# Linear attention and experts on one core: scores of two quads in five visits instead of six, the next batch's x turned earlier

## What is computed

```python
qf, kf = taylor_exp(q), taylor_exp(k)          # 16 heads, 16 features a head
A = tril(qf @ kf.T)                            # 512 x 512 for each batch and head
y = (A @ v) / (sum over past of qf . kf + EPS)
attention = y @ Wo.T
logits = xn @ Wg                               # 8 experts, the best two for each token
ffn = sum over top 2 of gate * (silu(xn @ W1[e].T) * (xn @ W2[e].T)) @ W3[e]
out = x + attention + ffn
```

## Time and profile before

| what | value |
|---|---|
| median of three runs | 640.49 us (639.61 to 642.61) |
| profiled execution | 641.93 us |
| its span, first to last instruction | 640.1 us |
| granted TensorE clock, mean | 0.998 |
| busy, share of the span | PE 96%, PEld 74%, DVE 70%, ACT 54%, POOL 56% |
| a batch of the attention stage (quad 0 of batch 3 to quad 0 of batch 4) | 35.15 us |

### The profile page before, as it was taken

The page is one execution under the profiler, slowest core; times in us unless marked ns, Lnnn a source line. Parts: engine busy times, 40 slices in busy tenths (PEclk is TensorE's granted clock), DMA queues, the critical chain, the costliest instruction groups (busy, mean ns, idle before and its releaser), DMA issues.

```text
span 640.1 us, 16670 instructions
## 1 busy us (share of the span) xinstructions
PE 615.1 (96%) x5181; PEld 475.5 (74%) x5181; DVE 450.3 (70%) x1134; ACT 348.0 (54%) x515; POOL 360.3 (56%) x453
## 2 busy tenths in 40 slices
PE   8899999999999999998899899999999999999995
PEld 8565665666666666655788788888888888888884
DVE  6876878787787776587787466666666667666663
ACT  3678878787878777775564233333333333333331
POOL 4265564737364654657167366566666666656645
PEclk9999999999999999999999999999999999999999
DMA  4753554545544444552953465656655656656553
GB/s 133 176 121 102 132 159 112 152 95 153 137 103 124 99 121 100 159 140 89 334 149 65 100 126 119 121 119 126 126 117 125 120 120 126 120 120 122 123 96 43
DMA packets 73347, 80.37 MB, mean 126 GB/s; under 512 B 12368, under 2 KB 61392, under 8 KB 73264
## 3 DMA queue, kind: packets, MB, share of 16 engines
q1 hardware_dynamic: 56144, 50.72, 30.1%
q0 software_dynamic: 16704, 28.12, 22.2%
q10 hardware_dynamic: 416, 0.46, 0.3%
HBM read 27.72 MB, written 22.95 MB: 79 GB/s over the span
## 4 chain that ended last, share of the span: by engine, by line
PE 43%; issue 26%; POOL 17%; DVE 8%; POOLq 2%; ACT 2%; DMA 0%; DVEq 0%; ACTq 0%
PE banks L1171 10%; POOL xg L544 9%; PE banks L1153 8%; PE banks L1191 7%; POOL out L570 6%; PE banks L1297 5%; PE banks L1200 4%; PE banks L1235 4%; POOL mark L556 3%; POOLq L554 2%; PE banks L1318 2%; PE banks L1220 2%; PE banks L1226 1%; ACT T L607 1%; DVE xTl L828 1%
## 5 line engine op out<-in xcount | busy, mean ns | idle before, releaser
L570 POOL DMA_INDIRECT out<-yo,xw x71 | 112.6, 1586 | 103.8 <-DVE yo L1100 99.9
L535 POOL TENSOR_SCALAR_AFFINE_SELECT T<-T 128x512 f32<-128x512 f32 x128 | 81.2, 646 | 108.6 <-ACT T L613 45.0
L1297 PE MATMUL banks<-w12h,xgh 128*128 x284 | 113.0, 398 | 3.4 <-DVE xgl L1078 3.3
L1297 PE MATMUL banks<-w12l,xgh 128*128 x284 | 111.4, 392 | 0.0
L1297 PE MATMUL banks<-w12h,xgl 128*128 x284 | 111.0, 391 | 0.0
L1112 DVE TENSOR_TENSOR hs<-banks,hs 128x512 f32<-128x512 f32 x71 | 49.1, 692 | 85.2 <-PE banks L1297 81.0
L706 ACT ACTIVATE sTh<-banks 128x512 fp32r<-128x512 f32 x71 | 42.4, 599 | 93.4 <-DVE banks L1088 76.8
L544 POOL DMA_INDIRECT xg<-xs_scr,glist x71 | 71.8, 1012 | 24.5 <-issue 19.7
L1171 PE MATMUL banks<-T,vau 128*17 128x512 f32 (+3 forms) x1024 | 75.5, 434 | 0.3 <-POOL T L535 0.3
L526 POOL DMA_INDIRECT xs_scr<-xb,slots x64 | 63.6, 994 | 19.0 <-issue 12.5
L1153 PE MATMUL banks<-Q,K 32*128 32x256 f32 (+2 forms) x1024 | 70.0, 358 | 2.0 <-DMA K<-Kt 1.8
(11 more groups left out here) (186 smaller groups left out, 1245.6 us busy)
## 6 DMA issues: line engine op xcount, KB each, us to landing
hq<-hs SPq DMA_DIRECT2D x244, 64.0 KB
w12r<-w SPq DMA_DIRECT2D x16, 512.0 KB, 4.4
Q<-Q SPq DMA_DIRECT2D x126, 64.0 KB, 2.4
out<-xa SPq DMA_DIRECT2D x16, 256.0 KB
w3r<-w SPq DMA_DIRECT2D x8, 512.0 KB, 7.1
K<-Kt SPq DMA_DIRECT2D x126, 32.0 KB
xa<-x SPq DMA_DIRECT2D x7, 512.0 KB, 4.8
xg<-xs_scr,glist POOLq DMA_INDIRECT x71
```

The source lines that it names most:

```text
L535: e.affine_select(out=v, in_=v, pattern=[[0, 4], [1, P]], compare_op=ALU.is_ge, fill=-1.0, base=0, channel_multiplier=-1).then_inc(s["g_mk ...
L570: e.indirect_dma_start(out, bass.IndirectOffsetOnAxis(xw[:, t % XR, NE:NE + 1].bitcast(U32), 0), yo[:, t % 2, :], None, compute_op=ALU.add ...
L1297: i = e.matmul(banks[:, 2 * (t % 2) + m, :], a[:, k, :], w[:, bass.ds(expert[t] * 4 + (2 * k + m), 1), :], start=(k == 0 and n == 0), stop ...
```

## The change

The last key block (3) moves from part 2 to part 1, where it fills the free 128 columns of the banks, now with matmuls of 128 columns. Part 2 then holds key block 2 alone, 256 columns, and is done for both quads of a pair at once, in the even quad: two quads have five visits. T1 and T2 have 4 x 512 columns each, the squares follow (`group` numbers the visits), and the masks of both quads in T2 are made in the even quad. The third visit of an even quad waits for the moves of both halves. The x steps of batches 2 to 7 go from `slot_b` to `slot_a` of quad 1, ahead of the second visit on all engines. yw moves to free space elsewhere, since T1 and T2 grew. In an odd quad the second send stands between the two T1 masks.

```diff
 def slot_a(n):
-    return [("C", 0, 0), ("f", 1, 6)] if n == 0 else []
+    b, qd = divmod(n, 4)
+    if n == 0:
+        return [("C", 0, 0), ("f", 1, 6)]
+    return [("x", b + 1, 0), ("x", b + 1, 1)] if qd == 1 and 0 < b < LAST else []
...
-        steps = [("x", b + 1, 0), ("x", b + 1, 1)] if b else [("v", 1, 0)]
+        steps = [] if b else [("v", 1, 0)]
...
+def group(n, part):
+    return 5 * (n // 2) + 3 * (n % 2) + part
...
-        T1 = r1.take("T1", 1536, F32, (4, 384))
-        T2 = r2.take("T2", 1536, F32, (4, 384))
-        yw = [r1.take("yw0", 512), r2.take("yw1", 512)]
+        T1 = r1.take("T1", 2048, F32, (4, 512))
+        T2 = r2.take("T2", 2048, F32, (4, 512))
+        ry = Region(Q1, Q1 + 1024)
+        yw = [ry.take(f"yw{u}", 512) for u in range(2)]
...
+            def masks(n):
+                b, qd = divmod(n, 4)
+                mask(n, T0[n % 2][:, :, 0:P], 0)
+                if sends_after(n, 0):
+                    send(*sends_after(n, 0))
+                mask(n, T1[:, :, 0:P], 1)
+                if sends_after(n, 1):
+                    send(*sends_after(n, 1))
+                mask(n, T1[:, :, 384:512], 1)
+                if qd == 2 and b < NBATCH - 2:
+                    root(b + 2)
+                if n % 2 == 0:
+                    mask(n, T2[:, :, 0:P], 2)
+                    mask(n, T2[:, :, 256:384], 2)
+                if sends_after(n, 3):
+                    send(*sends_after(n, 3))
...
             def squares1(n):
...
-                    e.activation(T1[:, 2 * h:2 * h + 2, :], banks[:, 2 * h:2 * h + 2, 0:384], ACT.Square, scale=0.25,
+                    e.activation(T1[:, 2 * h:2 * h + 2, :], banks[:, 2 * h:2 * h + 2, :], ACT.Square, scale=0.25,
...
-                squares2(n)
+                if n % 2 == 0:
+                    squares2(n)
...
-                jobs = (((0, 0, 512),), ((1, 0, 384),), ((3, 0, 256), (2, 256, 256)))[part]
-                for j, (jm, c0, w) in enumerate(jobs):
+                jobs = (((h, 0, 0, 512),), ((h, 1, 0, 384), (h, 3, 384, 128)), ((0, 2, 0, 256), (1, 2, 256, 256)))[part]
+                if part == 2:
+                    e.wait_ge(s[f"d_q{g}1"], MOVES * (b + 1))
+                    e.wait_ge(s[f"d_k{g}1"], MOVES * (b + 1))
+                for j, (hj, jm, c0, w) in enumerate(jobs):
...
-                scores(n, 2)
+                if n % 2 == 0:
+                    scores(n, 2)
```

More of the change, by code:

```diff
@@ L527, in send, with mask @@
                                          xb[b % 2][:, blk, :], None).then_inc(s[f"d_xs{b % 2}"], 16)
-            def mask(n):
-                b, qd = divmod(n, 4)
[L531 to L538, removed]
+            def mask(n, v, part):
+                e.wait_ge(s["a_s"], 2 * group(n, part) + 2)
+                e.affine_select(out=v, in_=v, pattern=[[0, 4], [1, P]], compare_op=ALU.is_ge, fill=-1.0, base=0,
+                                channel_multiplier=-1).then_inc(s["g_mk"], 1)
+            def masks(n):
+                b, qd = divmod(n, 4)
+                mask(n, T0[n % 2][:, :, 0:P], 0)
[12 more added lines that the diff above has]
+                    send(*sends_after(n, 3))
             def gather(t):
@@ L574, in gpsimd_program @@
             for n in range(NQ):
-                mask(n)
+                masks(n)
             done(e, "G", 0, 0)
-            e.wait_ge(s["p_s"], 6 * NQ)
+            e.wait_ge(s["p_s"], 5 * NQ)
             e.wait_ge(s["d_xs0"], 512)
@@ L595, in squares0 @@
                 for h in range(2):
-                    e.wait_ge(s["p_s"], 6 * n + h + 1)
+                    e.wait_ge(s["p_s"], 2 * group(n, 0) + h + 1)
                     if n >= 2 and h == 0:
@@ L603, in squares1 @@
                 for h in range(2):
-                    e.wait_ge(s["p_s"], 6 * n + h + 3)
+                    e.wait_ge(s["p_s"], 2 * group(n, 1) + h + 1)
                     if n and h == 0:
                         e.wait_ge(s["p_av"], n)
-                    e.activation(T1[:, 2 * h:2 * h + 2, :], banks[:, 2 * h:2 * h + 2, 0:384], ACT.Square, scale=0.25,
+                    e.activation(T1[:, 2 * h:2 * h + 2, :], banks[:, 2 * h:2 * h + 2, :], ACT.Square, scale=0.25,
                                  bias=1.0).then_inc(s["a_s"], 1)
@@ L611, in squares2 @@
                 for h in range(2):
-                    e.wait_ge(s["p_s"], 6 * n + h + 5)
-                    e.activation(T2[:, 2 * h:2 * h + 2, :], banks[:, 2 * h:2 * h + 2, P:512], ACT.Square, scale=0.25,
+                    e.wait_ge(s["p_s"], 2 * group(n, 2) + h + 1)
+                    e.activation(T2[:, 2 * h:2 * h + 2, :], banks[:, 2 * h:2 * h + 2, :], ACT.Square, scale=0.25,
                                  bias=1.0).then_inc(s["a_s"], 1)
@@ L1150, in scores @@
                             if j == 0 and p == 0 and r % 2 == 0 and n + part:
-                                e.wait_ge(s["a_s"], 6 * n + 2 * part + r // 2 - 1)
+                                e.wait_ge(s["a_s"], 2 * group(n, part) + r // 2 - 1)
                             rr = slice(32 * r, 32 * r + 32)
-                            i = e.matmul(banks[:, r, c0:c0 + w], K2[rr, g, h, jm * P:(jm + 1) * P], Q2[g][rr, h, p, 512 - w:512],
-                                         start=(p == 0), stop=(p == 1))
+                            i = e.matmul(banks[:, r, c0:c0 + w], K2[rr, g, hj, jm * P:(jm + 1) * P],
+                                         Q2[g][rr, hj, p, 512 - w:512], start=(p == 0), stop=(p == 1))
                             if j == len(jobs) - 1 and p == 1 and r % 2:
@@ L1166, in attend @@
                     e.wait_ge(s["c_b4"], 1)
-                for jm, w, v, mk in ((0, 512, T0[n % 2], 1), (1, 384, T1, 2), (3, 128, T2[:, :, 0:P], 3),
-                                     (2, 256, T2[:, :, P:384], 4)):
-                    e.wait_ge(s["g_mk"], 4 * n + mk)
+                mine = 256 * (n % 2)
+                for jm, w, v, mk in ((0, 512, T0[n % 2], (1, 6)), (1, 384, T1[:, :, 0:384], (2, 7)), (3, 128, T1[:, :, 384:512], (3, 8)),
+                                     (2, 256, T2[:, :, mine:mine + 256], (4, 5))):
+                    e.wait_ge(s["g_mk"], 8 * (n // 2) + mk[n % 2])
                     for r in range(4):
@@ L1330, in tensor_program @@
             e.wait_ge(s["v_te"], 1)
-            e.wait_ge(s["a_s"], 6 * NQ)
+            e.wait_ge(s["a_s"], 5 * NQ)
             expert_of(0)
```

## The result

The changed kernel takes 644.9 us in the median of 16 runs (641.27 to 648.32); the kernel before 640.43 (639.61 to 642.61, 16 runs). The ratio is 1.0068, 95% interval 1.0054 to 1.0082: slower, by 4.5 us. The forecast was 649.9 us, 9.4 us above the kernel before: the direction and the range held, and the size was more than twice too large. The profiled execution is one of the longest, with a span of 646.4 us against 640.1.

The account below looks back on a forecast made before the run. TensorE was taken to bound quads 0, 2 and 3, with a hole only in quad 1. With slow narrow jobs, +0.03 (batch 0), +9.7 (six batches) and -0.36 (batch 7) gave +9.4: 649.9 us, range 640.5 to 652.0.

Parts of the forecast that it names:

- The narrow job: Second visit: 8 matmuls of 128 columns, two rounds, 0.12 to 0.46 us; the upper was taken, visit 1.01 us.
- wide rate: Second visit: narrow rounds cost as wide score matmuls do, 0.12 us for two, visit 0.67 us; 642.7 us, chance 0.36.
- The wait for rk: Quad 1: t waits for the bank rk releases behind the x subtractions, starting at T+6.57; quad 0.52 us longer.
- the hole: Quad 1, between the second visit and t: TensorE idle 2.08 us with nothing left to do.
- The first rival: Second visit: narrow jobs run at the wide rate, extra waits eat the visits saved; 642.7 us, chance 0.36.
- Quad 0: Batches 1 to 6, first quad: longer second visit delays T1 squares and Q subtraction; +0.21 us, or +0.55 with slow narrow jobs.
- quad 2: Third quad of a batch: later T1 squares delay K copy and Kt subtraction; +0.42 us, or +0.76 with slow narrow jobs.
- quad 3: Last quad of a batch: second visit grows, third visit goes; -0.55 us, or -0.21 with slow narrow jobs.
- Batch 0: First batch, where x doesn't move: sum -0.65 us, or +0.03 with slow narrow jobs.
- Batch 7: Last batch: VectorE's lists hold TensorE, the last quad's third visit and mask wait go; -0.7 us, or -0.36.
- The rival that cashes the missing visits in quad 1: Quad 1: fast narrow jobs and rk not behind x subtractions give -0.55 us, six times; 636.3 us, chance 0.06.
- Late moves: Even quads: SP's K moves reach the third visit late, some 0.5 us a batch on top; 653 us, chance 0.06.

Follow-up runs that it names:

- places-first run: Changed kernel with VectorE doing places ahead of the x subtractions in quad 1 of batches 1 to 6: 634.64 us, ratio 0.9915; repeated on another chip, 0.9882.
- fillers: Changed kernel with six filler matmuls behind the second visit of quad 1 in batches 1 to 6: 640.42 us, ratio to the kernel before 1.0001.
- move alone: Kernel before with x moved ahead of the second visit of quad 1, six visits kept: 657.39 us, ratio 1.0265.
- five visits alone: Changed kernel with x left behind the second visit of quad 1, back in `slot_b`: 644.42 us, ratio 1.0068.
- narrow job three times: Changed kernel with the 128-column job of the second visit computed three times over: 664.62 us in its one run.
- half the fillers: Changed kernel with three filler matmuls instead of six in quad 1: 642.52 us, ratio 0.9996.
- six visits, moved, places first: Kernel before, six visits kept, with x moved and places ahead of the x subtractions on VectorE: 645.2 us, ratio 1.0028.

## Why the prediction was right and wrong

- **The narrow job** is the step of the forecast that failed: its cost was mis-sized. I took the upper bound, a second visit of 1.01 us, 0.34 more than at the wide rate, from f32 matmuls of the same width. The visit reads 0.72 us: the job costs 0.17, 0.05 above the lower bound of 0.12. That is also below the 0.8 us that the prediction named as the sign that the forecast is wrong. The nearest row in line, type and tiling (256-wide scores) was the right one; nearness in width was a bad guide. This alone moves the sum from +9.4 to about +3 (an estimate: +2.3 at the wide rate, and 0.05 for each of some 20 visits on the bound). The prediction read in the Trainium skill, page TensorE: Matmul & The Clock Gate, section Back-to-back issue gap, that narrow matmuls pay no penalty. Its 134 cycles for 128 columns, 0.056 us, are that section's figure for an isolated matmul. For a stream of weight loads and matmuls the section calls this too low at 128 columns, and gives about 81 ns. The runs here show 0.085 to 0.115 us for a round of four by TensorE's records, nearer to the second figure.
- **The wait for rk** was right in place and kind, so the prediction's second sign of being wrong (t within 0.5 us of the second visit's end) didn't show: t at T+6.42 (said: T+6.57), c at T+6.84 (T+7.01). Quad 1 is 9.86 us at the full clock; 10.05 was said. The places-first run, which moves rk forward, shows by its gain that rk is what t waits for.
- **What the hole does to the clock** was missing, a term put at nothing without a reason. The prediction gave the hole its 2 us and costed what lay behind it at the full clock, as if an idle TensorE were only idle. With the falls out (fillers) the change measures 1.0001; with them 1.0068. The extra waits that the forecast added up cost nearly nothing. So the forecast's sign is luck: it came out by a mechanism that the forecast didn't have. The first rival, 642.7 us, had the visit nearly right and is 2.2 us below the median; it lacked the falls and had the batches 0.5 us too long.
- **Quad 0** +0.17 (said, wide rate: +0.21), **quad 2** +0.22 (+0.42: the K copy comes where I had it, at T+5.61, but the Kt subtraction starts 1.06 us after it and not 1.28), **quad 3** -0.66 against the window of the earlier trace rows (-0.55). A batch without a fall is 35.25 us, 0.10 more than before, where I had +0.60 at the wide rate.
- **Batch 0** wins 1.2 us, from its first score visit to that of batch 1; 0.65 was said at the wide rate.
- **Batch 7** was right in kind: VectorE's lists hold t there, now for 2.12 us instead of 1.71, and the mask wait at the end is gone. I had -0.7 us; up to the first expert matmul it is +0.9 in the profiled run, of which the fall is about 1.4.
- **The rival that cashes the missing visits in quad 1** asked that rk be out of the way. It isn't, in the changed kernel; the places-first run is that rival made, 634.64 us (I had 636.3).
- **Late moves** didn't show: none of the third visits waits for a DMA.

## What to carry to other kernels

When a change takes work away from the engine that bounds, ask where it will idle instead, and for how long in one piece: on TensorE holes of 1.7 to 1.8 us in quad 1 were followed, in 11 of 18 cases over three profiles, by a fall of the clock that cost another 1.5 us. A hand-written order must be redone on all engines together; here the same five visits gave +0.7% with one order of two VectorE steps and -0.8% with the other (-1.2% on another chip). And where one cost has a bound from the same instruction and one from a look-alike, take the same instruction.

## What the runs showed of the hardware

- The granted clock fell to its lower level behind holes of TensorE, but not behind every one. In quad 1 of batches 1 to 6, in one profile each: behind 1.67 us four times of six (changed kernel), behind 1.8 us five of six (move alone) and two of six (five visits alone), behind 1.2 us (narrow job three times) and 0.8 us (half the fillers) never. At the stage's end it fell behind 2.12 us in the changed kernel and not behind an equal hole of the filled one; behind 1.6 us in six visits, moved, places first, and not behind 1.7 in the kernel before. So length alone doesn't decide, and what else does isn't shown. Filling the hole took the falls out of quad 1 in both kernels that were filled there.
- A fall cost 1.5 to 1.56 us in quad 1. Over the 16 runs of the changed kernel the mean clock goes from 0.995 in the shortest (641.27 us) to 0.983 in the longest (648.32), with 0.989 in the middle; the middle run of the kernel before and of the filled kernel has 0.997, of the move alone 0.981. The spread goes with the clock: a kernel with such holes is uneven as well as slow. But the kernel before isn't free of it: on the second chip its 23 runs go from 641.4 us to 650.41, at a mean clock of 0.987, and no trace here shows where it fell in that one.
- fp32r matmuls of 128 columns in four row groups cost 0.085 to 0.115 us a round of four by TensorE's records. With 24 of them in a row, ScalarE started on their banks about a microsecond later than those records account for, in even quads and most quads 3; in quad 1, with nothing behind them, it didn't. That stays open.
